# The second mixer moved wholly into the second message passing, and the edge network spread over four row groups

## The reference, cut to what matters

```python
w = ssp(edge_attr @ W_f1) @ W_f2 * (ssp(s0 @ W_s1) @ W_s2)      # a weight row of 512 for each edge
w1, w2, w3, w4 = jnp.split(w, 4, axis=-1)
x0e, x1e = split_irreps(x[edge_src])
out0 = w1 * x0e * sh0[:, None] + w4 * (jnp.einsum('eum,em->eu', x1e, sh1) / jnp.sqrt(3.0))
out1 = w2[:, :, None] * x0e[:, :, None] * sh1[:, None, :] + w3[:, :, None] * x1e * sh0[:, None, None]
out = jax.ops.segment_sum(merge_irreps(out0, out1), edge_dst, num_segments=N)   # then a linear map, + old x
# the mixer, 8 heads of 64:
q_, k_ = relu(q) + scale, relu(k) + scale          # q, k, v = x @ W_qkv.T
kv, k_sum = einsum('bnhe,bnhf->bhef', k_, v), sum(k_, axis=1)
z = 1.0 / (einsum('bnhe,bhe->bnh', q_, k_sum) + EPS)
out = (einsum('bnhe,bhef->bnhf', q_, kv) * z[..., None]).reshape(B, N, C) @ W_proj.T + b_proj
```

## Time and profile before

| | |
|---|---|
| median of three runs | 5622.0 us |
| the profiled execution's own time | 5678.81 us |
| its span | 5677.0 us |
| busy: PE, DVE, POOL, ACT | 4483.8, 3780.2, 3056.1, 2094.6 us |
| mean granted clock of PE | 0.889 of full |
| `edges1`, first to last `pws` product | 3304.7 to 5319 us |
| `merge1`, from its start to its last step | about 5341 to 5528 us |

### The profile page before, as it was taken

How to read it: one execution, slowest core, us unless ns; L and a number is a source line. 1 busy time by engine, 2 the same in 40 slices (tenths; PEclk the granted TensorE clock), 3 DMA queues, 4 the chain that set the end, 5 groups by cost and what they waited for, 6 DMA issues and landing times. The chain is left out here.

```text
span 5677.0 us, 60568 instructions
## 1 busy us (share of the span) xinstructions
PE 4483.8 (79%) x16401; PEld 2322.5 (41%) x16401; DVE 3780.2 (67%) x9307; ACT 2094.6 (37%) x4527; POOL 3056.1 (54%) x2739
## 2 busy tenths in 40 slices
PE   6402089977876888889696779999989999999797
PEld 3100046622222444445464634444444444444453
DVE  6300022278878888877476468888888888888784
ACT  1000012222222333311132556666666666666411
POOL 0777600066665666650033168778778777778300
PEclk9755599988888999899798989999999999999898
DMA  3000031166665666640565688898989888899624
GB/s 142 29 12 12 12 140 49 45 180 178 179 172 149 177 177 175 173 111 26 204 194 167 233 227 212 204 211 207 207 208 210 203 207 210 206 213 212 147 87 147
DMA packets 365424, 887.81 MB, mean 156 GB/s; under 512 B 67687, under 2 KB 119894, under 8 KB 364841
## 3 DMA queue, kind: packets, MB, share of 16 engines
q0 software_dynamic: 216464, 662.10, 47.0%
q1 hardware_dynamic: 135695, 194.16, 10.4%
q10 hardware_dynamic: 12954, 27.93, 1.3%
HBM read 663.41 MB, written 221.00 MB: 156 GB/s over the span
## 5 line engine op out<-in xcount | busy, mean ns | idle before, releaser
L1988 POOL DMA_INDIRECT mid_acc<-m_out,m_il x416 | 729.3, 1753 | 142.1 <-issue 121.6
L723 POOL DMA_INDIRECT s_krow<-mid_att_rows,s_ix x440 | 416.1, 946 | 675.7 <-ACT s_ix L759 441.9
L947 PE MATMUL m_pm<-m_vrow,m_same 128*128 128x512 f32 x880 | 528.2, 688 | 129.5 <-DVE m_vrow L890 92.6
L1978 POOL DMA_INDIRECT m_drow<-mid_drow,m_ig x416 | 446.8, 1074 | 289.0 <-issue 115.4
L797 PE MATMUL s_pq<-queries_q,s_same 128*128 x880 | 490.5, 693 | 110.9 <-DVE s_krow L737 40.6
L423 POOL DMA_INDIRECT mid_slots<-sort_rec,f_row x416 | 430.8, 1036 | 230.4 <-issue 128.4
L874 POOL DMA_INDIRECT m_vrow<-mid_att_rows,m_ix x440 | 417.9, 950 | 245.7 <-PE m_pm L948 134.2
L2288 PE MATMUL m_pm<-m_msg,m_same 128*128 128x512 f32 x832 | 495.5, 679 | 58.1 <-issue 26.5
L2280 PE MATMUL m_pws<-m_w,m_hid 32*128 32x512 f32 x832 | 483.5, 662 | 56.4 <-DVE m_hid L2033 29.5
L1978 POOL DMA_INDIRECT m_srow<-mid_srow,m_ig x416 | 436.0, 1048 | 127.0 <-issue 123.6
L2281 PE MATMUL m_pwf<-m_w,m_hid 32*128 32x512 f32 x832 | 484.3, 663 | 0.0
(11 more groups left out here) (377 smaller groups left out, 9168.9 us busy)
## 6 DMA issues: line engine op xcount, KB each, us to landing
mid_att_rows<-f_rows SPq DMA_DIRECT2D x75, 256.0 KB
mid_ys<-e_y SPq DMA_DIRECT2D x57, 256.0 KB
e_line<-in_src_lines POOLq DMA_DIRECT2D x52, 256.0 KB
m_line<-in_src_lines SPq DMA_DIRECT2D x104, 128.0 KB
g_q<-mid_qT SPq DMA_DIRECT2D x50, 256.0 KB, 3.7
g_a<-mid_acc SPq DMA_DIRECT2D x50, 256.0 KB, 2.9
keep_w<-in_w SPq DMA_DIRECT2D x16, 512.0 KB
s_krow<-mid_att_rows,s_ix POOLq DMA_INDIRECT x440
```

Source lines behind the costliest of these rows:

```text
L723: pool.indirect_dma_start(krow[:, k % SS, :], None, io["att_rows"][1], bass.IndirectOffsetOnAxis(ap=ix[:, k:k + 1], axis=0),).then_inc(s_g ...
L947: pe.matmul(pm[k % 4][:, 0:D], mine, vrow[:, k % SS, :], start=True, stop=True)
L1978: pool.indirect_dma_start(row, None, table, bass.IndirectOffsetOnAxis(ap=ig[:, n, t:t + 1], axis=0),).then_inc(s_g[t % S], 16)
L1988: pool.indirect_dma_start(io["acc1"][k % NACC], bass.IndirectOffsetOnAxis(ap=il[:, t:t + 1], axis=0), out[:, k % R, :], None, compute_op=A ...
```

## The change

In `edges1` the mixer no longer takes a whole pass for a node tile but half of one, eight tiles of edges ("slots" j = 0 to 7). The first 25 halves after the first make keys and values only (j = 1, 2 keys, 4, 5 values, two chunks of the product at each; 7 and the next 0 the products of keys and values). The half after them folds keys and values with the output weights. The next 25 halves load the normalised x a second time and make the queries (j = 1, 2), their sums by head (3, now 8 rows, not 128), the inverse on 8x128 values (4), its spread to all rows by a product with 8 rows (5), the division (5, DVE), the product with the folded weights and the biases (6, 7), and at the next half's 0 DVE adds the result to x in SBUF (`residual`). No queries go to HBM.

The edge network uses four groups of 32 rows instead of two: the hidden sums of tiles with an even place go to partitions 0 to 63, those with an odd place to 64 to 127, so softplus goes over 128x256 and not 64x512, and the factors of two neighbouring tiles come from different row groups. `both` issues them together: at the end of every odd tile k PE makes the factors of k+1 and k+2, after L2054 is done with tile k; the call of `weights(k+1)` at the start of each tile is gone.

`merge1` keeps the sum of the two `acc1`, its turn, the linear map, the addition to x and the statistics.

```diff
-        w_c, w_f1, w_2 = s.sb("w_c", [P, HID]), s.sb("w_f1", [HID, HID]), s.sb("w_2", [2 * HID, D])
+        w_c, w_f1, w_2 = s.sb("w_c", [P, HID]), s.sb("w_f1", [HID, HID]), s.sb("w_2", [4 * HID, D])
...
+        SLOTS, FOLD = EU // 2, NT + 1
...
+        ksum, z = s.sb("ksum", [P, KC, H]), key[0:H, 0:P]
+        two, extra = s.sb("two", [2, P]), s.sb("extra", [2, D])
+        w_p, kvw, kvT = W[:, :, D:2 * D], W[:, :, 2 * D:3 * D], key
+        heads = val[:].rearrange("p c n -> p (c n)")[0:H, 0:D]
...
+        HW = BW // 2
+        soft, hid = s.sb("soft", [4 * HID, HW]), s.sb("hid", [4 * HID, 2, HW])
...
+        PX = 4
+
+        def kv_node(h):
+
+            return h - 1 if 1 <= h <= NT else None
+
+        def q_node(h):
+
+            return h - FOLD - 1 if FOLD < h <= FOLD + NT else None
+
+        def slot(b, k):
+
+            return (EU * b + k) // SLOTS, k % SLOTS
...
+                def node_in(m, h):
+
+                    if m < NT:
+                        need(sp, s_px, PX * (m - 2) + 2)
+                    else:
+                        sp.wait_ge(s_px, PX * (min(m - 2, NT - 1)) + 2)
+                        need(sp, s_pq, m - 2 - NT + 1)
+                    n, cols = m % NT, slice(DH2 * h, DH2 * (h + 1))
+                    sp.dma_start(xT[:, m % 2, cols], io["xhT"][n][:, cols]).then_inc(s_x[m % 2], 16)
...
+                    h, part = g // ahead - 1, g % ahead
+                    if kv_node(h) is not None:
+                        node_in(kv_node(h), part)
+                    if q_node(h) is not None:
+                        node_in(NT + q_node(h), part)
+                    if g == ahead * (NT + 2) + 1:
+                        sp.wait_ge(s_px, PX * (NT - 1) + 1)
+                        sp.dma_start(w_p, io["w_proj"].rearrange("(c p) n -> p c n", p=P)).then_inc(s_wp, 16)
+                    if g == ahead * (NT + 3) + 1:
+                        sp.wait_ge(s_px, PX * NT)
+                        sp.dma_start(heads, io["heads"][:, :]).then_inc(s_heads, 16)
...
+                    h, j = slot(b, k)
+                    n = kv_node(h)
+                    if n is not None and j == 3:
                         vec.wait_ge(s_px, PX * n + 1)
-                        need(vec, s_qo, 32 * n)
-                        vec.tensor_scalar(q[:], px[:], 0.0, DH ** -0.5, ALU.max, ALU.add).then_inc(s_q, 1)
...
                         ins = vec.tensor_scalar(key[:], px[:], 0.0, DH ** -0.5, ALU.max, ALU.add)
...
-                    if n is not None and k == 14:
+                    if n is not None and j == 7:
                         kv_sums(n, 0)
-                    n = node_of(b - 1)
-                    if n is not None and k == 0:
+                    n = kv_node(h - 1)
+                    if n is not None and j == 0:
                         kv_sums(n, 1)
+                    if h == FOLD and j == 1:
+                        by_heads()
+                    n = q_node(h)
+                    if n is not None and j == 2:
+                        vec.wait_ge(s_pq, n + 1)
+                        vec.tensor_scalar(q[:], px[:], 0.0, DH ** -0.5, ALU.max, ALU.add).then_inc(s_q, 1)
+                    if n is not None and j == 4:
+                        vec.wait_ge(s_zq, n + 1)
+                        vec.reciprocal(z, z).then_inc(s_rq, 1)
+                    if n is not None and j == 5:
+                        vec.wait_ge(s_ps, n + 1)
+                        vec.tensor_tensor(q[:], q[:], px[:], ALU.mult).then_inc(s_qd, 1)
+                    n = q_node(h - 1)
+                    if n is not None and j == 0:
+                        residual(n)
...
+                def residual(n):
+
+                    vec.wait_ge(s_po, n + 1)
+                    x = keep.X[:, n, :]
+                    vec.tensor_tensor(x[:, 0:P], x[:, 0:P], px[:, 0:P], ALU.add)
+                    vectors = x[:, P:D].rearrange("p (u c) -> p c u", c=3)
+                    vec.tensor_tensor(vectors, vectors, px[:, P:D].rearrange("p (c u) -> p c u", c=3), ALU.add).then_inc(s_x1, 1)
...
+                residual(NT - 1)
+                vec.wait_ge(s_x1, NT)
...
+                for r in (0, 2 * HID):
+                    act.dma_start(w_2[r:r + HID, :], io["w_s2"][:, :]).then_inc(s_w, 16)
+                    act.dma_start(w_2[r + HID:r + 2 * HID, :], io["w_f2"][:, :]).then_inc(s_w, 16)
...
+                    act.activation(soft[:], ph[:, 0:HW], ACT.Abs).then_inc(s_soft, 1)
...
+                def mixer(b, k):
+                    h, j = slot(b, k)
+                    n = kv_node(h)
+                    if n is not None and j == 6:
+                        act.wait_ge(s_px, PX * n + 2)
                         act.wait_ge(s_val, n + 1)
...
+                    n = q_node(h)
+                    if n is not None and j == 4:
+                        act.wait_ge(s_pn, n + 1)
+                        need(act, s_ps, n)
+                        act.activation(z, px[0:H, 0:P], ACT.Copy, bias=1e-6).then_inc(s_zq, 1)
...
+                    place = 2 * (k % 2) + k % B // 2
                     for c in range(3):
...
+                    h, j = slot(b, k)
+                    n = kv_node(h)
+                    if n is not None and j in (1, 2):
+                        if j == 1:
                             if n == 0:
                                 pe.wait_ge(s_mixw, 16)
...
+                        rows(n, (2 * (j - 1), 2 * (j - 1) + 1), D)
+                    if n is not None and j in (4, 5):
+                        if j == 4:
                             pe.wait_ge(s_key, n + 1)
...
+                        rows(n, (2 * (j - 4), 2 * (j - 4) + 1), 2 * D)
+                    if n is not None and j == 7:
...
                         pe.wait_ge(s_kvs, 2 * n + 2)
-                        ins = pe.matmul(px[:, 0:P + 1], key[:, 3 * P:D], val[:, 3, :], start=True, stop=True)
-                    if k in (3, 8, 12, 14, 15):
+                        pe.matmul(px[:, 0:P + 1], key[:, 3 * P:D], val[:, 3, :], start=True, stop=True).then_inc(s_px, 1)
+                    if h == FOLD and j == 2:
+                        pe.wait_ge(s_kv, 2)
...
+                    if h == FOLD and j >= 4:
+                        c = j - 4
+                        if c == 0:
+                            pe.wait_ge(s_wp, 16)
+                            pe.wait_ge(s_kvT, 1)
+                        need(pe, s_kvw, c)
+                        pe.matmul(px[:], kvT[:, P * c:P * (c + 1)], w_p[:, c, :], start=True, stop=True).then_inc(s_kw, 1)
+                    n = q_node(h)
+                    if n is not None:
+                        query(n, j)
+
+                def rows(n, chunks, first):
+
+                    m = n % 2
+                    for c in chunks:
+                        ins = pe.matmul(px[:], xT[:, m, P * c:P * (c + 1)], W[:, c, first:first + D], start=c == 0, stop=c == KC - 1)
+                    if chunks[-1] == KC - 1:
                         ins.then_inc(s_px, 1)
+
+                def query(n, j):
+
+                    m = (NT + n) % 2
+                    if j in (1, 2):
+                        if j == 1:
+                            loads = sum(1 for x in range(NT + n + 1) if x % 2 == m)
+                            pe.wait_ge(s_x[m], 32 * loads)
+                            pe.wait_ge(s_kvw, KC)
+                            need(pe, s_x1, n)
+                        for k in (2 * (j - 1), 2 * (j - 1) + 1):
+                            for c in range(KC):
+                                ins = pe.matmul(px[:, P * k:P * (k + 1)], W[:, c, P * k:P * (k + 1)], xT[:, m, P * c:P * (c + 1)],
+                                                start=c == 0, stop=c == KC - 1)
+                        if j == 2:
+                            ins.then_inc(s_pq, 1)
+                    elif j == 3:
+                        pe.wait_ge(s_q, n + 1)
+                        for c in range(KC):
+                            ins = pe.matmul(px[0:H, 0:P], ksum[:, c, :], q[:, P * c:P * (c + 1)], start=c == 0, stop=c == KC - 1)
+                        ins.then_inc(s_pn, 1)
+                    elif j == 5:
+                        pe.wait_ge(s_rq, n + 1)
+                        if n == 0:
+                            pe.wait_ge(s_heads, 16)
+                        for c in range(KC):
+                            ins = pe.matmul(px[:, P * c:P * (c + 1)], heads[:, P * c:P * (c + 1)], z, start=True, stop=True)
+                        ins.then_inc(s_ps, 1)
+                    elif j in (6, 7):
+                        if j == 6:
+                            if n == 0:
+                                pe.wait_ge(s_extra, 16)
+                                pe.wait_ge(s_two, 2)
+                            pe.wait_ge(s_qd, n + 1)
+                            pe.matmul(px[:], two[:], extra[:], start=True, stop=False)
+                        for c in (2 * (j - 6), 2 * (j - 6) + 1):
```

(54 more changed lines are left out.)

167 lines of the change are left out of this document (50 added, 117 removed).

## The result

The changed kernel takes 5594.5 us (median of 4 runs, 5590.0 to 5598.4) against 5627.4 us for the kernel before on the same chip (4 runs, 5615.6 to 5634.2): ratio 0.9934, interval 0.9915 to 0.9952, 33 us less. The forecast was 41 us more, so its sign was wrong.

What follows compares the result with a forecast made beforehand. POOL was taken to bound edges1 at 4.78 of 4.89 us a tile, the chain over PE, ACT and DVE after the change. Terms -122 + 138 + 50 - 25 = +41 us on 5622 gave 5663 us, range 5515 to 5740.

Steps and rivals of the forecast that it cites:

- 41 us more: Whole kernel: the sum of -122, +138, +50 and -25, giving 5663 us.
- merge1, -122: In merge1: 11 us ahead of the first addition, then 2.12 us a tile on DVE, 65.5 us against 187.5.
- The chain in edges1: In edges1: late factors make DVE wait, so the chain replaces POOL as bound, at 5.12 and 5.35 us a tile.
- that POOL alone sets the pace of the kernel before: In edges1 before the change: POOL's transfers and issue gaps take 4.78 us of the 4.89 us a tile.
- I take 50: In edges1: at clock 0.95 PE's steps are 5% longer, 58 us over 50 halves, of which 50 were taken.
- the identity products, -25: In edges1's hidden: identity products alternate between two column groups and may overlap; -25 us, bounds 0 and -50.
- the chain itself, +138: In edges1: 0.23 us a tile with keys and values and 0.46 with queries over today's 4.89, 200 tiles each.
- the forecast of the stall: In edges1: DVE can start L2054 two tiles on only at 8.8 us, standing still 4.6 us in four tiles.
- 163 predicted for `edges1`: In edges1: the chain +138, the clock +50 and the identity products -25 taken together.
- the third: Rival, the two sides cancel: clock unchanged in effect, DVE takes up half the gaps; -12 us, 5600 to 5640, chance 20%.

Runs made afterwards that it cites:

- y1: The changed kernel with POOL's gather of drow replaced by a plain transfer of 128 consecutive rows (wrong rows, timing only): ratio 0.9893 to the kernel before.
- e5: The changed kernel with each tile's factor products issued at the start of the tile before it, four row groups kept: ratios 0.9789 and 0.9808 to the kernel before.
- e6: The kernel before with the mixer's four query pieces one tile later (tiles 1 to 4 instead of 0 to 3): ratio 0.9933 to the kernel before.

## Why the prediction was wrong

**merge1, -122: right.** Measured -127: 9.3 us from the first load to the first addition (5378.6 to 5387.9) where I took 11, a period of 2.1 as said.

**The chain in edges1: right in kind.** The bound moved from POOL to the chain over PE, ACT and DVE, by the steps named: the factors start as four, DVE waits at L2077 for ACT's factor, PE before `sums` for ACT's copy (y1 shows that the chain, not POOL, bounds it; e5 that the order is what costs). What the prediction said of the start, that POOL alone sets the pace of the kernel before, was nearly so: e6 gained 0.09 us a tile. A tile with keys and values came at 5.01 us where I had 5.12, with queries at 5.13 where I had 5.35.

**The step that failed: "I take 50", the clock.** I carried the grant of 0.95 from the kernel before into a chain that has none of the waits behind it. In the changed kernel PE runs at 1.00 in both halves, and the term is 0. The prediction even had a row with such a wait, 2.63 us and then two passes at half speed, and took the grant as a property of the stretch instead of its waits. e6 supports this by itself: 19 long gaps down to 5, 0.95 up to 0.98, with the same idle sum. Without this term the forecast would have been -9 us: the sign of the result, and less than a third of its size.

**Near, but by luck: the identity products, -25.** They fell from 0.99 to 0.56 us in each of 100 groups: -43, my outer bound of -50 nearly reached. I judged by the pair L2268 and L2269, and that pair (now L2384 and L2385) still runs one after the other, 0.55 us each; but the identity passes do overlap. What I had at nothing is the price of splitting the two products of 512 columns into four of 256: 2.19 us instead of 1.95, +24 in 100 groups. `hidden` as a whole fell by 0.19 us (2.94 to 2.75), so -19 where I had -25: two errors that nearly cancel. The Trainium skill ("TensorE: Matmul & The Clock Gate", on measured speedup against the span model) has outputs in different column groups run at once; the trace agrees for these passes, by a factor of 1.8 for two groups, and does not for L2384 and L2385.

**Mis-sized: the chain itself, +138, queries above all.** With `hidden` as measured my 5.12 and 5.35 become 5.07 and 5.30 us a tile (0.19 x 2 / 8 = 0.05 less); measured are 5.01 and 5.13. That is 13 us too much over the tiles with keys and values and 35 us over those with queries. In one group of the first kind the forecast of the stall is met: from the end of a message (3715.57) to L2077 two tiles on it takes 8.8 us, as laid out.
```profile
3715.29 0.28 DVE L2093 TENSOR_TENSOR m_msg<-m_msg,m_dot 128x128 f32<-128x128 f32 x1
...
3724.34 0.69 DVE L2077 TENSOR_TENSOR m_w<-m_pws,m_w 128x512 f32<-128x512 f32 x1 [2.63 <-issue]
```
By the starts of L2077, as a mean of 23 halves, the two groups of four tiles take 19.4 and 20.7 us with keys and values (laid out: 19.95 and 21.0) and 20.5 and 20.5 us with queries (21.3 and 21.5). So the second four with queries are furthest off; which of their steps is shorter I didn't test.

**Left out: +22.** Folding ran at 5.8 us a tile (69.5 us for 12, 11 us over 4.89), 2 us came in at the ends, and the kernel before took 4.87 us a tile over the whole stage (2025.5 / 416) and not 4.89, 9 us.

The terms then read: 163 predicted for `edges1`; less 50 (clock), 13 and 35 (the chain), and 6 (`hidden`) and 22 more: 93, against 92 measured. The rival closest to what happened is the third, with "clock unchanged in effect"; I had given it 20%. It has -12 where the stages show -35, and its other half, that DVE makes up for half of the gaps, no run tested.

## What to carry to other kernels

A granted clock below 1 belongs to rows and not to the stage: find the rows at the lower level and the waits in front of them, and ask whether the change keeps them, before carrying the number over. When a chain is lengthened under an engine that sets the pace, lay it out step by step; here that gave the time a tile to 0.06 us with keys and values and to 0.17 us with queries, once the clock and the length of `hidden` were put right. When products are split to run in parallel, price the split as well as the overlap: here it took back 0.24 of 0.43 us. And put the products that another engine waits for ahead of the bulk work of their engine: the same change with the factors issued first gained 2%, and with them last 0.7%.

## What the runs showed of the hardware

A plain transfer issued by POOL held it for 1.06 us, about as long as an indirect gather of 128 rows (1.04 to 1.20 in the rows shown). POOL's indirect transfers are no constants: the same three took 3.88 us in the kernel before and 4.09 in the first half of the changed one. PE's 128-column passes into two column groups start in pairs in either order of issue (0.56 and 0.57 us for eight against 0.99 in one group), while the pair L2384 and L2385 ran one after the other (0.55 us each). The grant of PE's clock did not follow PE's idle sum: 0.95 with 151.8 us idle in 1900, 0.98 with 150.9 in 1860, 0.99 with 384.9 in 2040.
